# A graph layer on one core: four projected chunks, a first step that ends in PSUM, five row buffers and transposes of the identity

## What is computed

```python
h = jnp.maximum(_layernorm(x, axis=-1), 0.0)
rowsum = adj.sum(axis=1)
d = jnp.where(rowsum > 0, rowsum ** (-0.5), 0.0)
support = (d[:, None] * adj * d[None, :]) @ h
x = x + jax.nn.relu(support @ W + b)
```

## Time and profile before

| | |
|---|---|
| time, median of 3 runs | 407.17 us (406.96 to 407.3) |
| the profiled execution | 406.59 us |
| its span, first to last instruction | 404.7 us |
| TensorE busy | 390.9 us (97%) |
| VectorE, ScalarE, GpSimd busy | 313.3, 289.0, 114.3 us |
| DMA queue of the data | 147.07 MB, 90.2% of 16 engines' span |

### The profile page before, as it was taken

The page is one execution under the profiler, slowest core; times in us unless marked ns, Lnnn a source line. Parts: engine busy times, 40 slices in busy tenths (PEclk is TensorE's granted clock), DMA queues, the critical chain, the costliest instruction groups (busy, mean ns, idle before and its releaser), DMA issues.

```text
span 404.7 us, 5156 instructions
## 1 busy us (share of the span) xinstructions
PE 390.9 (97%) x1760; PEld 324.6 (80%) x1760; DVE 313.3 (77%) x316; ACT 289.0 (71%) x283; POOL 114.3 (28%) x273
## 2 busy tenths in 40 slices
PE   3999899999999999999999999999999999999995
PEld 2888688888888888888888888888888888888884
DVE  5786677959796977868588697859579693899996
ACT  2699878787888888877877777878579755335532
POOL 2352524352441226422133432342233130000000
PEclk9999999999999999999999999999999999999998
DMA  8999999999999999999999799999999755487664
GB/s 283 405 421 421 421 422 419 421 419 420 424 419 421 421 419 422 420 418 421 417 423 414 287 385 407 417 421 358 409 341 384 306 202 209 183 348 249 207 195 168
DMA packets 22616, 147.39 MB, mean 364 GB/s; under 512 B 2624, under 2 KB 2880, under 8 KB 6208
## 3 DMA queue, kind: packets, MB, share of 16 engines
q1 hardware_dynamic: 22592, 147.07, 90.2%
HBM read 142.87 MB, written 4.19 MB: 363 GB/s over the span
## 4 chain that ended last, share of the span: by engine, by line
PE 93%; DMA 3%; ACT 2%; issue 1%; DVE 1%; SPq 0%; DVEq 0%
PE moved L718 21%; PE moved L719 21%; PE moved L720 21%; PE held L718 7%; PE held L720 7%; PE held L719 7%; PE held L688 4%; PE moved L688 3%; PE moved L671 2%; DMA nat<-in_adj 2%; PE moved L736 1%; DMA at<-in_x 1%; ACT turned L371 1%; ACT nat L351 0%; DVE acc L578 0%
## 5 line engine op out<-in xcount | busy, mean ns | idle before, releaser
L562 DVE SCALAR_TENSOR_TENSOR lo<-at,s,hi 128x1024 fp32r<-128x1024 f32 x112 | 141.4, 1279 | 26.9 <-ACT hi L364 26.7
L718 PE MATMUL moved<-hi,G 128*128 128x512 f32 x384 | 149.7, 390 | 1.8 <-DVE acc L578 1.8
L720 PE MATMUL moved<-hi,G 128*128 128x512 f32 x384 | 149.4, 389 | 0.0
L719 PE MATMUL moved<-lo,G 128*128 128x512 f32 x384 | 149.4, 389 | 0.0
L364 ACT ACTIVATE hi<-at,s 128x1024 fp32r<-128x1024 f32 x112 | 122.6, 1142 | 35.6 <-issue 34.7
L351 ACT ACTIVATE nat<-nat 128x2048 f32<-128x2048 f32 x64 | 122.3, 1912 | 29.3 <-DMA nat<-in_adj 29.3
L581 DVE TENSOR_TENSOR acc<-moved,acc 128x1024 f32<-128x1024 f32 x84 | 102.7, 1222 | 48.9 <-PE moved L720 48.7
L718 PEld LDWEIGHTS moved<-hi,G 128*128 128x128 f32 x384 | 72.1, 188 | 18.0 <-DVE acc L578 2.2
L720 PEld LDWEIGHTS moved<-hi,G 128*128 128x128 f32 x384 | 72.1, 188 | 15.0
L719 PEld LDWEIGHTS moved<-lo,G 128*128 128x128 f32 x384 | 72.1, 188 | 14.8
L480 POOL TENSOR_TENSOR row_sum<-part 128x1 f32<-128x1 f32 x32 | 15.5, 484 | 167.5 <-ACT nat L351 167.4
(11 more groups left out here) (57 smaller groups left out, 234.0 us busy)
## 6 DMA issues: line engine op xcount, KB each, us to landing
nat<-in_adj SPq DMA_DIRECT2D x64, 1024.0 KB, 10.4
at<-in_adj_t SPq DMA_DIRECT2D x64, 1024.0 KB, 9.1
nat<-in_x_t SPq DMA_DIRECT2D x4, 512.0 KB, 4.7
turned<-in_x_t SPq DMA_DIRECT2D x4, 512.0 KB, 5.6
out<-nat SPq DMA_DIRECT2D x4, 512.0 KB, 4.7
at<-in_x SPq DMA_DIRECT2D x3, 512.0 KB, 6.8
turned<-in_x SPq DMA_DIRECT2D x3, 512.0 KB, 12.7
out<-turned SPq DMA_DIRECT2D x3, 512.0 KB, 5.0
```

The lines of the kernel that those rows point to most:

```text
L562: nc.vector.scalar_tensor_tensor(out=lo[g % RING][:, tiles, :], in0=at[g % LA][:, tiles, :], scalar=s[:, j:j + 1], in1=hi[g % RING][:, til ...
L718: nc.tensor.matmul(into[:, f, :], big, hi[g % RING][:, t, :], start=begins, stop=False)
L719: nc.tensor.matmul(into[:, f, :], big, lo[g % RING][:, t, :], start=False, stop=False)
L720: mm = nc.tensor.matmul(into[:, f, :], small, hi[g % RING][:, t, :], start=False, stop=ends)
```

## The change

Chunk 4 is no longer among the chunks done ahead: it is turned in step 4 and projected in step 5, and chunks 5, 6 and 7 move to steps 6, 9 and 11. Chunks 2 and 3 are copied by VectorE (before: 3 and 4). Step 0 takes panels 2 to 7 first and panels 0 and 1 last. Products 0, 1 and 3 lie in `held`, product 2 in a moved pair; their split is in the order 0, 2, 3, 1, that of chunk 1 only during step 0. There are five row buffers. The DMA order puts row loads between the `x` chunks, leaves chunk 4 out, and puts slot 2 behind row loads 4 and 5. Before the first chunk TensorE transposes the identity 32 times into a moved pair. The scratch memory that the builder reserves for descriptors is set to 1024.

```diff
-AHEAD = 5
-BY_VECTOR = [3, 4]
-TURNED_IN = {5: 5, 6: 7, 7: 10}
-LOADING = {k - 4 if c < 7 else k - 3: c for c, k in TURNED_IN.items()}
+AHEAD = 4
+BY_VECTOR = [2, 3]
+TURNED_IN = {4: 4, 5: 6, 6: 9, 7: 11}
+LOADING = {k - 3: c for c, k in TURNED_IN.items()}
+RAW_ORDER = [0, 2, 3, 1] + list(range(AHEAD, RAW))
+WARM = 32
 def panel_order(k):
-    return list(range(HELD, NP)) + list(range(HELD)) if k == LAST else list(range(NP))
+    return list(range(HELD, NP)) + list(range(HELD)) if k in (0, LAST) else list(range(NP))
-    LN = 3
+    LN = 5
         for c in range(AHEAD):
-            use(("turn", c), c % ROT, *turned_signal(c))
-        use(("project", AHEAD - 1), AHEAD % ROT, raw_ready, AHEAD)
+            use(("turn", c), (c + 1) % ROT, *turned_signal(c))
+        use(("project", 2), 1, raw_ready, raw_count(2))
         def chunk_product(c):
-            return held[c % 2] if c < AHEAD - 1 else pair_of(("project", c))
+            return held[c % 3] if c in (0, 1, 3) else pair_of(("project", c))
         # sync
+            load_nat(0)
             load_x(2)
+            load_nat(1)
             load_x(3)
-            for m in range(2 * WIDTHS[0]):
-                load_nat(m)
-                if m == 1:
-                    load_x(4)
+            load_nat(2)
+            load_nat(3)
             load_slot(0)
             load_slot(1)
-            load_slot(2)
...
                 for m in NATS[g]:
                     load_nat(m)
+                if g == 0:
+                    load_slot(2)
                 if g + 3 < len(SLOTS):
                     load_slot(g + 3)
         # scalar
             take_turned(1)
             round_raw(0)
-            take_turned(2)
-            sum_nat(1)
-            sum_nat(2)
-            round_raw(1)
-            sum_nat(3)
+            for m in range(1, 2 * WIDTHS[0]):
+                sum_nat(m)
+            round_slot(0)
             round_raw(2)
-            round_slot(0)
+            round_slot(1)
             round_raw(3)
-            round_slot(1)
-            round_raw(4)
             for g, (k, q, _) in enumerate(SLOTS):
+                if g == 1:
+                    round_raw(1)
+                    round_slot(g + 2)
                 for m in NATS[g]:
                     sum_nat(m)
-                if g + 2 < len(SLOTS):
+                if g != 1 and g + 2 < len(SLOTS):
                     round_slot(g + 2)
         # gpsimd
+            mean_of(3)
             rstd_of(0)
-            mean_of(3)
-            mean_of(4)
             scale_of(0)
+            scale_of(1)
             rstd_of(1)
-            scale_of(1)
         # vector
             centre(3)
+            take_turned(2)
             rest_of_raw(0)
-            take_stats(4)
-            centre(4)
             take_turned(3)
-            rest_of_raw(1)
-            take_turned(4)
+            for c in range(2):
+                subtract(0, c)
             rest_of_raw(2)
-            for g in range(2):
-                for c in range(2):
-                    subtract(g, c)
-                rest_of_raw(3 + g)
+            for c in range(2):
+                subtract(1, c)
...
                     subtract(g + 2)
+                if g < 2:
+                    rest_of_raw(RAW_ORDER[2 + g])
         # tensor
             pe.wait_ge(consts_made, 1)
+            for _ in range(WARM):
+                nc.tensor.transpose(moved[0][:, 0, 0:P], ident[:, :], ident[:, :])
             turn(0)
...
             project(2)
-            turn(4)
             project(3)
-            project(4)
-    nc = bacc.Bacc("TRN2", target_bir_lowering=False, num_devices=1)
+    nc = bacc.Bacc("TRN2", target_bir_lowering=False, num_devices=1, dynamic_dma_scratch_size=1024)
```

More of the change, by code:

```diff
@@ L106, in pieces, with raw_count @@
     return sum(2 if NARROW[k] else 1 for k, _, _ in SLOTS[:g + 1]) if g >= 0 else 0
+def raw_count(c):
+    return RAW_ORDER.index(c) + 1
 def at_least(eng, sem, value):
@@ L175, in h @@
         def h(c):
-            if c == AHEAD - 1:
-                flat = acc[:, NP - HELD - 1, :, :].rearrange("p f r -> p (f r)")
-            elif c < AHEAD:
+            if c < AHEAD:
                 e = c % 2
@@ L270, in build @@
                     c = PROJECTING[k]
-                    signal, count = (raw_ready, c + 1) if c < RAW else (hW_ready, c - RAW + 1)
+                    signal, count = (raw_ready, raw_count(c)) if c < RAW else (hW_ready, c - RAW + 1)
                     use(("project", c), gathered % ROT, signal, count)
@@ L507, in _ @@
                 scale_of(j)
-                if j in (3, 5, 7):
+                if j in (3, 5):
                     rstd_of((j + 1) // 2)
@@ L536, in rest_of_raw @@
             def rest_of_raw(c):
-                dve.wait_ge(raw_hi_made, c + 1)
+                dve.wait_ge(raw_hi_made, raw_count(c))
                 tiles = slice(BW * c, BW * (c + 1))
@@ L676, in project @@
                 half = BW // 2
-                if c >= AHEAD - 1:
+                if c == 3:
+                    pe.wait_ge(raw_ready, raw_count(0))
+                elif c >= 2:
                     pair_free(("project", c))
-                elif c >= 2:
-                    pe.wait_ge(raw_ready, c - 1)
                 signal, count = turned_signal(c)
@@ L696, in multiply @@
                     if k == 0:
-                        pe.wait_ge(raw_ready, AHEAD - HELD + i)
+                        pe.wait_ge(raw_ready, raw_count((3, 1)[i]))
                 else:
@@ L711, in multiply @@
                         if j < RAW * BW:
-                            pe.wait_ge(raw_ready, j // BW + 1)
+                            pe.wait_ge(raw_ready, raw_count(j // BW))
                         else:
```

## The result

| | before | changed |
|---|---|---|
| median | 407.06 us (4 runs) | 411.77 us (411.19 to 411.93, 4 runs) |
| ratio | | 1.0112, 95% interval 1.0091 to 1.0132 |
| profiled execution's span | 404.7 us | 409.4 us |

The medians lie 4.7 us apart; +4.2 and 411.4 were forecast. The page of the changed kernel: TensorE is busy 4.7 us longer, by the 32 transposes (5.2) and a stretch at half rate, less the first projection, which now runs at full rate; chunk 4's turn and projection are counted in both kernels. No other engine's busy time moved by more than 2.2 us.

The account below looks back on a forecast made before the run. TensorE and transfers both full; start -4.95, chunk 4's work +4.33, waits +4.9 gave +4.3; by gate B alone +4.2, which was taken: 411.4 us median, range 407.6 to 413.2.

Parts of the forecast that it names:

- the gates: Two kinds of place where late row loads reach TensorE through in-order queues of ScalarE and VectorE, about 5.55 and 5.1 us after landing.
- The start: Start of the large multiply, forecast at 27.1 us, 4.95 us sooner than before.
- The transposes: The 32 identity transposes before chunk 0: forecast to take 5.7 us, bounds 3.5 and 7.0, ending at 7.3.
- Step 0: First step of the large multiply: fourth panel to wait 2.5 us and fifth 0.9, behind VectorE's copies.
- fifth case: Slower still, 414 us: multiply starts over 3 us later than 27.1, or half rate in step 0's waits; 5%.
- gate B: Third panel of a chunk-turning step, awaiting ScalarE's copy behind row sums and hi; new 1.7 us wait in step 4.
- Gate A: Sixth panel of a step, awaiting a gather behind row sum and split; waits 1.4 us in step 1, 0.5 in step 2.
- the landing: Arrival of row load 24's data, forecast 1.7 us sooner, so summed from 122.8 instead of 124.50.
- case 3: Transfers go faster, 2.41 us per MB, row load 24 landing by 119.1: 407.9 us, no difference; 8%.
- Case 2: The turned chunk's copy in step 4 is not late, only the sixth-panel gather waits hold: 409.7 us; 13%.
- Case 4: Faster, 404.5 us: sooner landings plus ScalarE's chain in step 0 shorter by 2.5, no wait left; 12%.

## Why the prediction was right

**What bounds it: right.** Data and TensorE run side by side, and a saving at the start is worth only what the gates let through. Two tests show it from opposite ends: 3.7 us taken out of step 0 changed nothing while the gates stood, and opening the gates alone gave 3.8.

**The start.** 27.1 forecast, 27.27 measured. The transposes: 5.7 us forecast, 5.21 here and 6.48 in the version with reordered list, transposes and five buffers, both inside the bounds of 3.5 and 7.0.

```profile
1.67 5.21 PE L760 MATMUL moved<-ident 128*128 128x128 f32 x32 [1.67 <-POOL ident L453]
```

**Step 0.** Waits of 2.5 and 0.9 forecast. The first was 2.3. The second did not come: the stretch at half rate, 8 starts 0.2 us too far apart, made TensorE itself 1.6 us later, and the pair was free by then. With 0.6 of small gaps, most of them at first matmuls, it lost 4.5 where 3.4 was forecast. That clock stretch was in the prediction only as part of the fifth case; it came, and cost nothing, being ahead of the gates: one of the four executions had a mean granted clock of 0.999, too high for such a stretch, and with 411.93 us was no faster than the others. That the total of the forecast's terms (4.3) comes near 4.7 is partly luck, since the stretch stands in for a wait; the sum by gate B alone doesn't need it. The kernel before had also lost 2.5 by the distances of starts and not 2.1, as a wait in brackets lacks 0.16.

**Gate A.** Step 1: 1.4 forecast, 0.9 measured, since TensorE came later; the matmul started at 68.14, forecast 67.45. Step 2: 0.5 forecast at the sixth panel, 0.7 measured at the fifth. Here the mechanism was another: the statistics of chunk 4, which I had put on no path, delayed the gather by 1.3 us. A step that moves brings all its instructions, also those that it issues two steps earlier. But they added little. Without them the forecast wait at the sixth panel would have come, as an estimate 0.4 us: hi from 86.84 lets the gather of 89.21 end at 90.4, and the panel would have been due at 90.05. The version that turns the chunk in step 5 has no statistics there, and waits in step 2 at the fifth and the sixth panel.

**Gate B.** Right in place, releaser and reason; 1.7 forecast, 1.35 measured. The turned copy was done 0.6 later than forecast (TensorE at 128.52, not 127.9). The term that was off is the landing: 1.0 us sooner and not 1.7. 0.3 of the difference is there at row load 0 already, summed from 10.92 where the rate gives 10.6:

```profile
10.92 1.91 ACT L361 ACTIVATE nat<-nat 128x2048 f32<-128x2048 f32 x1 [2.12 <-DMA nat<-in_adj]
```

What made it late isn't shown, and it need not be the new order of issue: without the transposes, but with the same transfers, row load 0 is summed from 9.87 and row load 24 from 122.98, 0.2 from the forecast's 122.8. A term of this size is no better known than one landing repeats. It is the whole error of the time in the profile: from gate B on the forecast had 275.9 us of work to the last matmul (403.8 - 127.9), and 275.7 passed (404.26 - 128.52).

**The cases.** Faster transfers (case 3) are refuted by 421 GB/s with five buffers, in the changed kernel and in the one before with nothing else changed. Case 2 is refuted by the wait of 1.35 at gate B. Case 4, the faster one, needed step 0 to give way and the landings too; clearing step 0 without the landings is the experiment with slots 2 and 3, and it brought nothing.

**Where the expected gain of the change went.** It saves 4.8 at the start and pays 4.3 for chunk 4 later, which leaves 0.5. It then waits or runs slow for 5.2 us more than before (4.7 + 0.5). The order of the row sums on ScalarE is worth 3.8 of the time, and with it mended the losses of step 0 another 2.9; together that is more than 5.2 because the kernel before has losses of its own, 2.5, of the same kind.

## What to carry to other kernels

When two resources are both full, time saved at the start is worth nothing until the next place where the slower one hands over; find that place (the landing, and every instruction between it and the waiting engine) before pricing anything ahead of it. The cheapest cure here was neither more buffers nor an earlier start but the order of one engine's list: what another engine waits for goes ahead of what nobody needs yet. An edit ahead of such a gate should be tried again after the gate is opened, for its worth can change from nothing to 2.9 us, as that of slots 2 and 3 did. And a landing read from one execution is good to half a microsecond here, no better.

## What the hardware showed that I had not expected

TensorE's clock fell to half (1.2 GHz, 0.50 granted) after single waits of some two microseconds in the middle of dense work: after 2.3 us in the changed kernel, 2.4 with chunk 4 one step later, 2.1 with the row sums behind, 2.5 with the transposes alone; about 8 matmuls then start 0.43 us apart and some 1.6 us are lost. It did not fall after 1.9 us in the kernel before, 2.1 without the transposes, 2.1 with slots 2 and 3 ahead (at 64.16) and 2.3 with the row loads later. The length of the wait alone doesn't decide: between 2.1 and 2.3 us both happened. The Trainium skill (TensorE: Matmul & The Clock Gate, "What's actually happening") says that the gate follows how busy the array has been recently. That the clock fell only behind waits agrees with it; which of two equal waits is followed by half rate no run here lets one foresee.
